# Routed feed-forward stages as one block each, and a sparse attention output summed in four parts

## The chip, the cores and the metric
The kernel runs on one core of one Trainium2 chip. The metric is device time in microseconds (us) of one execution. The core has five engines with queues of their own: TensorE (PE; its weight loads are listed as PEld), VectorE (DVE), ScalarE (ACT), GpSimd (POOL) and SyncE (SP), which issues most DMAs. They are ordered by semaphores alone.

## The reference
A perceiver with four layers. The state `x` is 16 batches of 64 latents of width 128, so 1024 tokens; the context is 16 x 1601 x 128. Each layer adds a cross-attention, a self-attention and a feed-forward stage to `x`, each on a normalised copy. Four of the twelve stages matter here; everything is float32.

- **Feed-forward 1**: 8 experts, width 128 to 512 to 128 with ReLU and biases. Softmax of the router's logits, the best two experts of each token, their probabilities shared out to sum to one, and a capacity of 256 places an expert: a token whose place in an expert's queue is beyond it loses that expert.
- **Feed-forward 2**: 8 experts that are one 128 x 128 matrix and a bias each; the best two of each token are summed with weight one.
- **Feed-forward 3**: 8 experts 128 to 128 to 128 with SiLU, weighted by the router's probability (the best two), and a shared gated expert whose output is scaled by a sigmoid of each token.
- **Cross-attention 3** (sparse): 16 heads of 8; of each query's 1601 scores only the 32 largest take part in the softmax.

```
first two experts:  p = softmax(logits); keep = top-2(p)
out = x + sum_e coef[token, e] * (act(xn @ W1[e] + b1[e]) @ W2[e] + b2[e])
```

## The kernel before
The whole state lives in on-chip memory: `c.x` is 128 partitions x 8 tiles x 128, `c.xn` the normalised copy, `c.xnT` its transpose. `perceiver` runs the twelve stages one after another. A stage is a row of blocks (`nc.Block()`): in a block each engine has its own list of instructions, and at a block's end all engines meet at a barrier. There is no planner: the order on each engine is the order in which the code was written, and waits on semaphores tie the lists together. `layernorm` is the first block of each stage; SP loads the stage's small weights in it and waits for all of them before the barrier.

**Routed stages.** `stage_l1_ffn` is norm, `turn_all` (transposes of the router's weights and of the first bias), `route`, `add_expert_bias` and `experts`. `route` is one block: TensorE makes logits for all 1024 tokens (L2500), VectorE finds the coefficients in some 20 dependent small steps on 128 x 64 (L2521 to L2562, `Link` makes each wait for the one before), ACT takes one Exp between (L2515), and with a capacity TensorE counts the picks between (L2508, L2509) and VectorE sums the counts over the tiles. `add_expert_bias` is two blocks: the coefficients are transposed one tile at a time, and multiplied by the bias rows (L2578), and VectorE adds the product (L2584). `experts` is one block with a hardware loop on each engine, two experts in an iteration. A *half* is one expert on 512 tokens: `up(k)` (L2640) makes C banks of hidden values, ACT applies the function (L2670), `down(k)` (L2649) makes the output, VectorE adds it to `x` weighted by the coefficient (L2696), four instructions. Weights lie in two slots, loaded by L2611 and L2613; a slot is loaded again once its expert is done. In the first stage the first weights are also transposed (L2635, copy by VectorE at L2686), and each expert's bias and coefficients are copied out for the loop (L2681, L2682). `stage_l2_ffn` transposes 8 matrices in `turn_all`, routes, adds the bias and then runs a block: TensorE multiplies a tile by all 8 matrices (L2752), two tiles ahead, and VectorE adds the 8 results one after the other (L2761). `stage_l3_ffn` routes, runs `experts` with C = 1, and then the shared expert in a block of its own (L2791 to L2813).

**Sparse cross-attention** (`topk_cross_attention`). 128 steps, each two heads of one batch. In step s VectorE searches the 32 largest of 1601 scores (`fold` L1144 and L1146, `find` L1160, `drop` L1165), ACT and GpSimd turn the scores of step s-1 into weights, and TensorE transposes and sums those of s-2, after the scores of s+1. `turn_u` (L946) transposes a step's normalised sum into bank `psZ`, and ACT copies it to `UT` (L1059). Every 16 steps two batches are complete: `sums` (L951) multiplies all 16 heads' `UT` by the output weights into the same bank, 32 instructions, and VectorE adds the result (`add`, L1183) right after it has inverted that step's sum (L1179). Steps 1 to 4 and 9 to 12 of each 16 also make the next batch's keys (L902, L987). The order of the products and of the add:

```
                        for q in range(4):
                            values(t, q)
                        if t and t % (2 * TB) == 0:
                            sums(t // (2 * TB) - 1)
```

Of the kernel before, what the change touches and what calls it, by code (L numbers as in the profile page):

```python
# [783 lines left out]
def topk_cross_attention(c, N, QT, WkT, bk):  # L784
# [9 lines left out]
    LISTS = 7  # L794
    with ExitStack() as st:
# [21 lines left out]
        UT = c.sb(st, "UT", [128, H, 2, S])  # L817
# [12 lines left out]
        slot = {use: u for u, use in enumerate(uses)}  # L830

# [26 lines left out]
        with nc.Block() as block:  # L858
# [25 lines left out]
            def _(pe):  # L884
# [63 lines left out]
                def sums(p):  # L948
                    pe.wait_ge(ut_ready, 2 * TB * (p + 1) + ONE)
                    for h in range(H):  # L950
                        last = pe.matmul(psZ[:, 128:256], UT[:, h, :, :], N[:, h, :], start=(h == 0),  # L951
                                         stop=(h == H - 1))
                    last.then_inc(y_ready, 1)
# [4 lines left out]
                for s in range(T + 2):  # L958
                    if s + 1 < T:
                        scores(s + 1)  # L960
                    t = s - 2
                    if t in keyed:
                        project(*keyed[t])
# [5 lines left out]
                    if t >= 0:  # L969
                        turn(t, 2)  # L970
                        turn(t, 3)
                        for q in range(4):
                            values(t, q)
                        if t and t % (2 * TB) == 0:
                            sums(t // (2 * TB) - 1)
                turn_u(T - 1)
                sums(NT - 1)

            @block.scalar
            def _(act):  # L980
# [73 lines left out]
                def copy_ut(t):  # L1054
                    p, b, n = t // (2 * TB), t // TB, t % TB
                    act.wait_ge(u_turned, t + 1 + ONE)
                    if t % (2 * TB) == 0 and p:
                        act.wait_ge(y_ready, p + ONE)
                    act.activation(UT[:, 2 * n:2 * n + 2, b % 2, :],  # L1059
# [76 lines left out]
            def _(dve):  # L1136
# [44 lines left out]
                def add(p):  # L1181
                    dve.wait_ge(y_ready, p + 1 + ONE)
# [4 lines left out]
                for s in range(T + 2):  # L1187
# [12 lines left out]
                    if s < T:  # L1200
                        find(s, 2, KP)
                    if s + 1 < T:
# [8 lines left out]
                add(NT - 1)  # L1211
                dve.wait_ge(y_added, NT + ONE)
# [1253 lines left out]
def route(c, st, Wr, br, weights, cap=None):  # L2466

    nc = c.nc
    coef = c.sb(st, "coef", [128, NT, E])
    with ExitStack() as s:
        p = c.sb(s, "p", [128, NT, E])
        rest = c.sb(s, "rest", [128, NT, E])
        first = c.sb(s, "first", [128, 2, NT, E])
        rank = c.sb(s, "rank", [128, NT, E])
        m = c.sb(s, "m", [128, 2, NT, 1])
        r = c.sb(s, "r", [128, NT, 1])
        tri = c.sb(s, "tri", [128, 128])  # L2480
        off = c.sb(s, "off", [128, 2, NT + 1, E])
        ps = c.ps(s, "logits", [128, NT * E])
        pc = c.ps(s, "counts", [128, 4, NT * E])
        made, order, logits, sub, expd = (c.sem(n) for n in ("made", "order", "logits", "sub", "expd"))
        picked, counted, done = c.sem("picked"), c.sem("counted"), c.sem("done")
        with nc.Block() as block:
            @block.gpsimd
            def _(pool):
                link = Link(pool, made)

                link(pool.iota(rank[:], pattern=[[0, NT], [-1, E]], base=E, channel_multiplier=0,
                               allow_small_or_imprecise_dtypes=True))
                link(pool.memset(tri[:], 1.0))
                link(pool.affine_select(out=tri[:], in_=tri[:], compare_op=ALU.is_ge, fill=0.0, base=0,
                                        pattern=[[1, 128]], channel_multiplier=-1))

            @block.tensor
            def _(pe):
                for t in range(NT):
                    last = pe.matmul(ps[:, t * E:t * E + E], c.xnT[:, t * 128:t * 128 + 128], Wr,  # L2500
                                     start=True, stop=True)
                last.then_inc(logits, 1)
                if cap:
                    pe.wait_ge(picked, 1 + ONE)
                    pe.wait_ge(made, 3 + ONE)
                    for k in range(2):
                        f = first[:, k].rearrange("p t e -> p (t e)")
                        pe.matmul(pc[:, k, :], tri[:], f, start=True, stop=True)  # L2508
                        last = pe.matmul(pc[:, 2 + k, :], c.ones[:], f, start=True, stop=True)  # L2509
                    last.then_inc(counted, 1)  # L2510

            @block.scalar
            def _(act):
                act.wait_ge(sub, 1 + ONE)
                act.activation(p[:], p[:], ACT.Exp).then_inc(expd, 1)  # L2515

            @block.vector
            def _(dve):
                link = Link(dve, order)
                dve.wait_ge(logits, 1 + ONE)  # L2520
                link(dve.tensor_copy(p[:].rearrange("p t e -> p (t e)"), ps[:]))  # L2521
                if br is not None:
                    link(dve.tensor_tensor(p[:], p[:], bc(br, [128, NT, E]), ALU.add))
                link(dve.reduce_max(r[:, :, 0], p[:], axis=X))
                dve.tensor_tensor(p[:], p[:], bc(r[:], [128, NT, E]), ALU.subtract).then_inc(sub, 1)
                dve.wait_ge(expd, 1 + ONE)
                link(dve.reduce_sum(r[:, :, 0], p[:], axis=X))
                link(dve.reciprocal(r[:, :, 0], r[:, :, 0]))
                link(dve.tensor_tensor(p[:], p[:], bc(r[:], [128, NT, E]), ALU.mult))
                link(dve.tensor_copy(rest[:], p[:]))  # L2530
                dve.wait_ge(made, 3 + ONE)
                for k in range(2):
                    f = first[:, k]
                    link(dve.reduce_max(m[:, k, :, 0], rest[:], axis=X))
                    link(dve.tensor_tensor(f, rest[:], bc(m[:, k], [128, NT, E]), ALU.is_equal))
                    link(dve.tensor_tensor(f, f, rank[:], ALU.mult))
                    link(dve.reduce_max(r[:, :, 0], f, axis=X))
                    link(dve.tensor_tensor(f, f, bc(r[:], [128, NT, E]), ALU.is_equal))
                    if k == 0:
                        link(dve.scalar_tensor_tensor(out=rest[:], in0=f, scalar=-2.0, in1=rest[:],  # L2540
                                                      op0=ALU.mult, op1=ALU.add))
                if cap:

                    link(dve.tensor_tensor(r[:], m[:, 0], m[:, 1], ALU.add))
# [1030 lines left out]
```

## Time and profile before

| | |
|---|---|
| time, median of 3 runs | 4493.35 us (4491.63 to 4499.15) |
| the profiled execution's time | 4484.32 us |
| its span | 4482.6 us |
| busy share PE / DVE / ACT / POOL | 79% / 76% / 63% / 23% |
| mean granted TensorE clock | 0.912 of 2.4 GHz |
| feed-forward 1, from its norm to the next one | 1552.2 to 1729.6 us |
| feed-forward 2 | 2634.9 to 2693.3 us |
| sparse cross-attention, steps | about 2740 to 4240 us |
| feed-forward 3, to its last add | 4391.7 to 4477.0 us |

The profile is one execution, recorded by the hardware. Times of rows count from its span's start. The shares are averages over stages that are bound by different engines, so each stage has to be read by itself. A TensorE row is one hardware instruction: a float32 product is two of them. "Idle before" is how long the engine stood before a row's work, and what released it.

### The profile page before, as it was taken

How to read it: one execution, taken by the hardware profiler on the slowest of the kernel's cores; microseconds unless marked ns; L12 is line 12 of the kernel's file. 1: busy time of each engine (PE TensorE's matmuls, PEld its weight loads, DVE VectorE, ACT ScalarE, POOL GpSimd, SP SyncE). 2: the span in 40 equal slices, each digit the busy share in tenths (PEclk: the TensorE clock that was granted, in tenths of full speed). 3: DMA queues.
4: the chain of work that ended last, by engine and by line, in shares of the span. 5: the costliest groups of instructions: out<-in, count | busy, mean ns of one | idle time of the engine just before them, and what ended most of it. 6: DMA issues, size and time to landing. Idle time of an engine off the chain costs nothing. (4 is left out here: it accounts for less than half of the span.)

```text
span 4482.6 us, 71801 instructions
## 1 busy us (share of the span) xinstructions
PE 3525.9 (79%) x25855; PEld 2832.6 (63%) x25855; DVE 3418.4 (76%) x5489; ACT 2808.6 (63%) x4637; POOL 1033.6 (23%) x1056
## 2 busy tenths in 40 slices
PE   6345649999999677999999875777777777777796
PEld 3334338999998355999999753555555555555574
DVE  5675767777777624877777557999999999999643
ACT  3113517666666423666666425999999899999732
POOL 0000502121110201211211002444434443444310
PEclk9556769999999788999999887999999999999897
DMA  8752011011110102101110001000000000000000
GB/s 277 95 84 78 5 48 36 30 42 33 30 38 8 26 28 65 38 30 30 40 35 23 22 6 40 16 16 30 16 16 16 16 30 16 16 16 8 20 4 17
DMA packets 186564, 161.25 MB, mean 36 GB/s; under 512 B 8220, under 2 KB 174316, under 8 KB 186220
## 3 DMA queue, kind: packets, MB, share of 16 engines
q1 hardware_dynamic: 182828, 142.83, 12.1%
q10 hardware_dynamic: 3392, 13.93, 0.9%
q8 instruction: 203, 3.33, 0.3%
q14 instruction: 141, 1.16, 0.1%
HBM read 127.36 MB, written 20.20 MB: 33 GB/s over the span
## 5 line engine op out<-in xcount | busy, mean ns | idle before, releaser
L538 PEld LDWEIGHTS psU<-ctxN,ST 128*128 128x128 f32 x6656 | 853.7, 191 | 98.2 <-issue 39.4
L538 PE MATMUL psU<-ctxN,ST 128*128 128x129 f32 x6656 | 868.1, 275 | 20.4 <-issue 20.4
L1160 DVE MAX8 top<-pairs 128x8 f32<-128x801 f32 (+1 forms) x512 | 709.2, 1406 | 4.5
L624 ACT ACTIVATE ST<-ST 128x512 f32<-128x512 f32 (+1 forms) x832 | 513.1, 625 | 167.1 <-DVE ST L726 163.2
L1125 POOL TENSOR_TENSOR P<-P,EX 128x1601 f32<-128x1601 f32 x128 | 459.5, 3590 | 582.5 <-ACT P L1035 582.5
L935 PE MATMUL psU<-ctxN,PT 128*128 128x129 f32 (+1 forms) x3328 | 432.0, 281 | 202.0 <-ACT PT L1043 202.0
L726 DVE TENSOR_TENSOR ST<-ST,psB 128x512 f32<-128x512 f32 (+1 forms) x832 | 556.4, 677 | 3.2 <-PE psB L557 3.2
L712 DVE TENSOR_TENSOR psA<-psA,ST 128x512 f32<-128x512 f32 x640 | 446.8, 698 | 137.5 <-ACT ST L616 70.4
L935 PEld LDWEIGHTS psU<-ctxN,PT 128*128 128x128 f32 (+1 forms) x3328 | 394.3, 193 | 226.3 <-ACT PT L1043 226.3
L1165 DVE MATCH_REPLACE8 pairs<-top,pairs 128x801 f32<-128x801 f32 (+1 forms) x384 | 482.4, 1256 | 0.0
L913 PE MATMUL psS<-KT,stat 128*128 128x512 f32 (+1 forms) x1024 | 390.4, 525 | 15.9 <-DVE pairs L1144 15.1
L526 PE MATMUL psS<-statL,ctxH 128*128 128x512 f32 x832 | 393.2, 473 | 5.0 <-ACT ST L619 2.5
L616 ACT ACTIVATE ST<-psS,key_bias 128x512 f32<-128x512 f32 (+1 forms) x416 | 284.2, 683 | 145.2 <-PE psS L526 140.2
L619 ACT ACTIVATE ST<-psS 128x512 f32<-128x512 f32 (+1 forms) x416 | 246.9, 593 | 165.9 <-PE psS L526 160.5
L923 PE MATMUL psT<-ident,P 128*128 128x128 f32 (+1 forms) x1664 | 256.6, 283 | 95.5 <-ACT KT L987 71.2
L526 PE MATMUL psS<-statH,ctxH 128*128 128x512 f32 x832 | 331.2, 398 | 0.0
L526 PE MATMUL psS<-statH,ctxL 128*128 128x512 f32 x832 | 328.0, 394 | 0.0
L913 PEld LDWEIGHTS psS<-KT,stat 128*128 128x128 f32 x1024 | 190.5, 196 | 212.1 <-issue 211.1
L923 PEld LDWEIGHTS psT<-ident,P 128*128 128x128 f32 (+1 forms) x1664 | 192.4, 144 | 166.0 <-ACT KT L987 85.4
L656 POOL CAST ctxH<-ctxM 128x1601 fp32r<-128x1601 f32 x30 | 45.6, 1521 | 1011.5 <-DVE ctxM L685 1011.5
L1043 ACT ACTIVATE PT<-psT 128x512 f32<-128x512 f32 (+1 forms) x512 | 240.7, 511 | 17.5 <-PE psT L923 17.5
L994 ACT ACTIVATE SS<-psS 128x1601 f32<-128x1601 f32 x128 | 192.4, 1503 | 74.2 <-PE psS L913 73.7
(502 smaller groups left out, 6261.4 us busy)
## 6 DMA issues: line engine op xcount, KB each, us to landing
ctxT<-ctxT_scratch SPq DMA_DIRECT2D x48, 800.5 KB, 4.7
ctxN<-in_ctx SPq DMA_DIRECT2D x48, 768.0 KB
ctxT_scratch<-trn ACTq DMA_DIRECT2D x16, 800.5 KB
nat<-in_ctx SPq DMA_DIRECT2D x16, 768.0 KB
dist_scratch<-dd SPq DMA_DIRECT2D x8, 800.5 KB
skewed<-in_ctx SPq DMA_DIRECT2D x8, 768.0 KB
ctx_late<-in_ctx SPq DMA_DIRECT2D x8, 768.0 KB
room<-skewed SPq DMA_DIRECT2D x28, 201.0 KB, 4.2
```

Of the source, the lines that this page charges most:

```text
L526: last = pe.matmul(psS[:, i % RING, :], x[:, u // 2 % 2, o:o + 128], q[:, p % 2, heads, queries], start=(n_pass == 0), stop=(n_pass == 2))
L538: last = pe.matmul(psU[:, q, 0:D + 1], ST[0:n, i % SLOTS, q * 128:q * 128 + 128], ctxN[0:n, j, k, 0:D + 1], start=(k == 0 and q % 2 == 0), ...
L616: act.activation(ST[0:n, i % SLOTS, :], psS[0:n, i % RING, :], ACT.Identity, bias=key_bias[0:n, col:col + 1]).then_inc(copied, 1)
L624: act.activation(ST[0:n, i % SLOTS, :], ST[0:n, i % SLOTS, :], ACT.Exp).then_inc(exp_done, 1)
L712: dve.tensor_tensor(psA[:], psA[:], cell, ALU.max).then_inc(folded, 1)
L726: dve.tensor_tensor(cell, cell, psB[0:n, :], ALU.subtract).then_inc(shifted, 1)
L913: last = pe.matmul(psS[:, o:o + w], stat[:, b % 2, 2 * n:2 * n + 2, :], KT[:, b % 2, o:o + w], start=True, stop=True)
L923: last = pe.transpose(psT[0:w, j, (k % 4) * 128:(k % 4) * 128 + 128], P[:, t % 2, o:o + w], c.ident[:])
L935: last = pe.matmul(psU[:, 0:D + 1], PT[0:w, t % 2, k, :], ctxN[0:w, t // TB % 2, k, 0:D + 1], start=(k == 0), stop=(k == NC - 1))
L1125: pool.tensor_tensor(P[:, j, :], P[:, j, :], EX[:, j, :], ALU.mult).then_inc(p_ready, 1)
L1160: dve.max(top[:, j, 8 * n:8 * n + 8], pairs[:, j, 0:width]).then_inc(listed, 1)
L1165: dve.match_replace(pairs[:, j, 0:width], top[:, j, 8 * n:8 * n + 8], pairs[:, j, 0:width], LOW).then_inc(listed, 1)
```

## The change
Each routed stage becomes the norm and one block, without a loop. `route` turns into a class, `Router`, whose parts are called from each engine's list. TensorE goes on with products of the first experts while VectorE finds the coefficients; the bias is an output like another one, in the middle of the list. ACT takes over the copies of transposed weights. Expert 0 and 1 of the first stage, and all of the last stage's, are loaded in the norm; the other six of the first stage at the start of the block, each with its own place and semaphore. `hT` has three slots for two. In the last stage the shared expert comes first, in two halves, and GpSimd multiplies its gate. In the second stage the adds start with the coefficients, and the bias is added after two tiles.

In the sparse attention the output of 16 heads is made in four parts of four heads. For the first seven batch pairs they are made in steps 5, 6, 7 and 13 of the next 16, ahead of that step's transposes; each is added by VectorE after the third search. `UT` is doubled, since it is still read while the next one is filled. The transpose of U in the same step waits for the add, which reads its bank. For the last pair the four parts follow each other at the end.

```
-    with ExitStack() as s:
-        p = c.sb(s, "p", [128, NT, E])
...
+class Router:
...
+    def choose(self, dve):
+        p, rest, first, m, r, off, wide = self.p, self.rest, self.first, self.m, self.r, self.off, [128, NT, E]
+        link = Link(dve, self.order)
+        dve.wait_ge(self.logits, 1 + ONE)
+        if self.br is None:
+            link(dve.tensor_copy(p[:].rearrange("p t e -> p (t e)"), self.ps))
+        else:
+            link(dve.tensor_tensor(p[:], self.ps.rearrange("p (t e) -> p t e", e=E), bc(self.br, wide), ALU.add))
...
+def add_weighed(dve, c, bank, half, weight, y_added):
+
+    for t in range(4):
+        tt = half * 4 + t
+        last = dve.scalar_tensor_tensor(out=c.x[:, tt, :], in0=bank[:, t * 128:t * 128 + 128], scalar=weight(tt),
+                                        in1=c.x[:, tt, :], op0=ALU.mult, op1=ALU.add)
+    last.then_inc(y_added, 1)
```

The first stage, norm and TensorE's and ACT's lists:

```
+        layernorm(c, [(g[:], d["L1_ffn_gate_w"]), (b1n[:], d["L1_ffn_fc1_b"].rearrange("e a (q p) -> (e a q) p", p=128)),
+                      (b2[:], d["L1_ffn_fc2_b"].rearrange("e a d -> (e a) d"))] + weights(0) + weights(1))
...
+                for e in range(2, E):
+                    for out, src in weights(e):
+                        sp.dma_start(out, src).then_inc(loaded[e], 16)
...
+                def up(i):
+                    e, half = i // 2, i % 2
+                    pe.wait_ge(copied, turn_use["w", e] + 1 + ONE)
+                    for q in range(C):
+                        if i:
+                            pe.wait_ge(h_ready, C * (i - 1) + q + 1 + ONE)
+                        pe.matmul(psH[:, q, :], w1T[:, e, q, :], c.xnT[:, half * 512:half * 512 + 512],
+                                  start=True, stop=True).then_inc(h_made, 1)
...
+                turn(("w", 0))
+                pe.wait_ge(small_copied, 2 + ONE)
+                route.make_logits(pe, Wr[:])
+                turn(("w", 1))
+                up(0)
+                up(1)
+                route.count(pe)
+                for i in range(UNITS):
+                    down(i)
+                    if i + 2 < UNITS:
+                        up(i + 2)
+                    if i % 2 == 0 and i // 2 + 2 < E:
+                        turn(("w", i // 2 + 2))
+                    if i == BIAS_FROM - 1:
+                        for half in range(2):
+                            turn(("coef", half))
+                        for half in range(2):
+                            bias(half)
...
+                copy(("w", 0))
+                act.wait_ge(small_copied, 2 + ONE)
+                copy(("w", 1))
+                route.exponentiate(act)
+                rectify(0)
+                rectify(1)
```

The second stage's and the last stage's TensorE lists:

```
+                route.make_logits(pe, Wr[:])
+                product(0)
+                product(1)
+                pe.wait_ge(route.coef_ready, 1 + ONE)
...
+                for t in range(2, NT):
+                    product(t)
...
+                last.then_inc(gates_made, 1)
+                route.make_logits(pe, Wr[:])
+                shared_up(0)
+                up(0)
+                shared_up(1)
+                up(1)
+                output(0)
+                output(1)
+                for i in range(UNITS):
+                    if i + 2 < UNITS:
+                        up(i + 2)
+                    output(2 + i)
```

The sparse attention:

```
+        summed = {PAIR * (p + 1) + n: (p, g) for p in range(NT - 1) for g, n in enumerate((5, 6, 7, 13))}
...
-                    if t % (2 * TB) == 0 and t:
-                        pe.wait_ge(y_added, t // (2 * TB) + ONE)
+                    if t + 1 in summed:
+                        p, g = summed[t + 1]
+                        pe.wait_ge(y_added, PARTS * p + g + 1 + ONE)
...
+                    if t in summed:
+                        sums(*summed[t], t - 1)
...
-                        if t and t % (2 * TB) == 0:
-                            sums(t // (2 * TB) - 1)
                 turn_u(T - 1)
-                sums(NT - 1)
+                for g in range(PARTS):
+                    sums(NT - 1, g, T)
...
-                        if s > 3 and (s - 3) % (2 * TB) == 0:
-                            add((s - 3) // (2 * TB) - 1)
...
                         find(s, 2, KP)
+                    if s - 2 in summed:
+                        add(*summed[s - 2])
```

## Rows read from the trace of the kernel before

**Rows 1.** Windows: us, busy (instructions) by engine, PEclk, DMA share, GB/s.
```profile
1552.00:1590.00 38.00, 14.84 (x60) 11.38 (x61) 17.52 (x86) 4.70 (x8) 0.74 (x3) 0.55 0.07 21
1590.00:1729.60 139.60, 121.42 (x672) 85.80 (x670) 24.42 (x86) 43.98 (x64) 0.00 (x0) 0.98 0.08 25
4408.00:4460.00 52.00, 37.41 (x160) 24.67 (x160) 19.02 (x72) 14.69 (x20) 0.00 (x0) 0.83 0.07 20
3300.00:3512.00 212.00, 157.10 (x938) 115.36 (x939) 207.78 (x259) 195.75 (x286) 91.23 (x96) 0.99 0.08 24
1100.00:1300.00 200.00, 197.73 (x1416) 181.80 (x1416) 158.17 (x256) 136.74 (x233) 41.23 (x29) 1.00 0.12 38
```

**Rows 2.** Timeline, feed-forward 1, routing: start, us, engine, line, operation, count [idle before].
```profile
1559.69 3.55 PE L2500 MATMUL logits<-Wr,xnT 128*128 128x8 f32 x16 [0.74 <-PEq L229]
1563.28 0.23 DVE L2521 COPY p<-logits 128x64 f32<-128x64 f32 x1 [4.11 <-PE logits L2500]
...
1568.88 0.07 DVE L2547 MEMSET off<- 128x8 f32 x1
...
1576.10 0.23 DVE L2562 TENSOR_TENSOR coef<-coef,p 128x64 f32<-128x64 f32 x1
...
1589.65 1.11 PE L2635 MATMUL psX<-ident,w1n 128*128 128x128 f32 x4 [5.38 <-DMA w2n<-in_L_ffn_fc_w]
```

**Rows 3.** Timeline, feed-forward 1, the experts' loop.
```profile
1591.64 6.04 PE L2640 MATMUL psH<-xnT,w1T 128*128 128x512 f32 x8 [0.88 <-DVE w1T L2686]
...
1628.10 3.69 PE L2640 MATMUL psH<-xnT,w1T 128*128 128x512 f32 x8 [2.04 <-DVE w1T L2686]
...
1652.43 7.31 PE L2649 MATMUL psY<-w2n,hT 128*128 128x128 f32 x64
...
1662.21 3.69 PE L2640 MATMUL psH<-xnT,w1T 128*128 128x512 f32 x8 [2.03 <-DVE w1T L2686]
...
1728.00 1.13 DVE L2696 SCALAR_TENSOR_TENSOR x<-psY,ce,x 128x128 f32<-128x128 f32 x4 [2.44 <-PE psY L2649]
```

**Rows 4.** Timeline, feed-forward 2: transposes, router, adds.
```profile
2641.40 3.38 PE L236 MATMUL turn<-ident,We 128*128 128x128 f32 x8
...
2649.21 0.23 DVE L2521 COPY p<-logits 128x64 f32<-128x64 f32 x1 [4.11 <-PE logits L2500]
...
2654.37 0.23 DVE L2560 TENSOR_TENSOR coef<-first 128x64 f32<-128x64 f32 x1
...
2668.10 24.68 DVE L2761 SCALAR_TENSOR_TENSOR x<-psE,coef,x 128x128 f32<-128x128 f32 x64 [4.31 <-PE psE L2752]
```

**Rows 5.** Timeline, feed-forward 3: a table load in the loop, the last adds.
```profile
4424.67 1.28 ACT L2670 ACT_TABLE_LOAD   x1 [3.23 <-DVE ce L2682]
4425.97 0.60 ACT L2670 ACTIVATE hT<-psH 128x512 f32<-128x512 f32 x1
...
4474.86 2.16 DVE L2813 SCALAR_TENSOR_TENSOR x<-psY,sg,x 128x128 f32<-128x128 f32 x8 [3.88 <-PE psY L2798]
```

**Rows 6.** Timeline, sparse attention: first and 125th reciprocal, an add, a turn of U.
```profile
2776.03 0.15 DVE L1179 RECIPROCAL li<-psU 128x1 f32<-128x1 f32 x1
...
2958.15 0.29 DVE L1183 TENSOR_TENSOR x<-x,psZ 128x128 f32<-128x128 f32 x1 [1.28 <-PE psZ L951]
2958.36 0.08 DVE L1165 MATCH_VALUE_LOAD pairs<-top,pairs 128x8 f32 x1
...
3109.67 1.83 DVE L1160 MAX8 top<-pairs 128x8 f32<-128x1602 f32 x1
3110.13 0.33 PE L946 MATMUL psZ<-ident,U 128*128 128x128 f32 x1 [0.97 <-ACT U L1051]
...
4209.48 0.15 DVE L1179 RECIPROCAL li<-psU 128x1 f32<-128x1 f32 x1
...
4235.55 3.84 PE L951 MATMUL psZ<-N,UT 128*128 128x128 f32 x32 [0.37 <-ACT UT L1059]
```

**Rows 7.** Source view of L2613: its eight 256 KB and eight 64 KB transfers.
```profile
DMA to landing us min/median/max: 1.8/2.6/4.9
```

**Rows 8.** The page's costliest groups: GpSimd's product in the sparse attention.
```profile
L1125 POOL TENSOR_TENSOR P<-P,EX 128x1601 f32<-128x1601 f32 x128 | 459.5, 3590 | 582.5 <-ACT P L1035 582.5
```

More of the change, by code:

```diff
@@ new lines, in rectify @@
+                def rectify(i):
+                    if i >= SLOTS:
+                        act.wait_ge(y_ready, place["unit", i - SLOTS] + 1 + ONE)
+                    for q in range(C):
+                        act.wait_ge(h_made, C * i + q + 1 + ONE)
+                        act.activation(hT[:, i % SLOTS, q, :], psH[:, q, :], ACT.Relu, bias=b1[:, i // 2, q:q + 1]
+                                       ).then_inc(h_ready, 1)
+                act.wait_ge(small_turned, 1 + ONE)
+                act.activation(Wr[:], small[:, 0:E], ACT.Copy).then_inc(small_copied, 1)
@@ new lines, in _ @@
+                act.activation(b1[:].rearrange("p e q -> p (e q)"), small[:, E:E + 32], ACT.Copy).then_inc(small_copied, 1)
+                copy(("w", 0))
[6 more added lines that the diff above has]
+                    if i + 2 < UNITS:
+                        rectify(i + 2)
+                    if i % 2 == 0 and i // 2 + 2 < E:
+                        copy(("w", i // 2 + 2))
+                    if i == BIAS_FROM - 1:
+                        for half in range(2):
+                            copy(("coef", half))
@@ L2744, in stage_l2_ffn, with _, product @@
         flat = WeT[:].rearrange("p e d -> p (e d)")
         with nc.Block() as block:
+            @block.gpsimd
+            def _(pool):
+                route.make_tables(pool)
             @block.tensor
             def _(pe):
[L2748 removed]
+                def product(t):
+                    pe.wait_ge(copied, 2 + ONE)
                     if t >= 2:
[L2750 removed]
+                        pe.wait_ge(added, E * (t - 1) + ONE)
@@ new lines, in _ @@
+                for t in range(2, NT):
+                    product(t)
+            @block.scalar
+            def _(act):
+                act.wait_ge(small_turned, 1 + ONE)
+                act.activation(Wr[:], small, ACT.Copy).then_inc(small_copied, 1)
+                for n in range(2):
+                    act.wait_ge(turned, n + 1 + ONE)
+                    act.activation(flat[:, 512 * n:512 * n + 512], psX[:, n, :], ACT.Copy).then_inc(copied, 1)
+                route.exponentiate(act)
+                for n in range(2):
+                    act.wait_ge(turned, use_at["coef", n] + 1 + ONE)
+                    act.activation(cT[:, 4 * n:4 * n + 4, :].rearrange("p t d -> p (t d)"), psX[0:E, n, :], ACT.Copy
+                                   ).then_inc(copied, 1)
@@ L2767, in stage_l3_ffn @@
 def stage_l3_ffn(c):
     nc, d = c.nc, c.dram
+    UNITS = 2 * E
+    SLOTS = 3
+    outputs = [("shared", 0), ("shared", 1)] + [("unit", i) for i in range(UNITS)]
     with ExitStack() as st:
@@ new lines, in shared @@
+                def shared(half):
+                    act.wait_ge(shared_made, half + 1 + ONE)
+                    act.activation(upper[:, half, :], psG[:, 1, :], ACT.Copy).then_inc(up_ready, 1)
+                    act.activation(gate[:, half, :], psG[:, 0, :], ACT.Silu).then_inc(silu_ready, 1)
+                route.exponentiate(act)
+                act.wait_ge(gates_made, 1 + ONE)
+                act.activation(sg[:], psg, ACT.Sigmoid).then_inc(gated, 1)
+                shared(0)
+                silu(0)
```

567 lines of the change are left out of this document (301 added, 266 removed).

## The prediction
> **What bounds the kernel now.** I read the windows view first, by stage. The first routed stage has two halves: up to 1590 us TensorE is busy 14.8 of 38 us at a granted clock of 0.55, and no engine is half busy; from 1590 to 1729.6 it is busy 121 of 139.6 us at 0.98, so there it is the bound, with holes [rows 1]. The last stage's experts are worse: 37 of 52 us at 0.83. The sparse cross-attention is bound by VectorE (208 of 212 us) [rows 1]. Then the timeline. In the routing part [rows 2] the reader sees a relay: logits, some 20 small VectorE steps, counts, coefficients, bias, and only then weights that are issued when the bias is added; the products that need none of this begin at 1591.64 [rows 3]. In the loop, two experts (four halves of 512 tokens) take 1662.21-1628.10 = 34.11 us [rows 3].
>
> **First routed stage (8 experts, 16 halves).** The new block starts later than the old routing, for the norm's block now waits for 1 MB of weights. A 256 KB transfer among four landed after 1.8 to 4.9 us [rows 7]. Now the first of four is issued at about 1553.3 (1552.2 and three small issues), the last 1.6 us later; with 4.5 us for the last I get 1559.3, and 0.4 us of barrier: 1559.7, where the small transposes stood at 1558.5. Cost 1.1 (bounds 0 and 3.5). The Trainium skill (DMA: Bandwidth & Descriptors, "Anatomy of one DMA — SWDGE (gpsimd) path") gives 2.0 us plus bytes over 436 GB/s, for 1 MB 4.4 us from the first issue; that would make this cost nothing, and what it says is for another way of issuing.
>
> From there TensorE: small transposes and the first expert's (1.5), logits 3.55 [rows 2], to 1564.7. A turn of four is 1.1 at the low clock [rows 2]. VectorE needs 1568.88-1563.28+0.1 = 5.7 us to its picks, but ACT now copies expert 1's weights and loads the Exp table (1.28 [rows 5]) after them, so Exp ends at 1568.0 instead of 1565.8: picks at 1572.7. Meanwhile TensorE turns expert 1 (1.1), does half 0 (8 instructions, 6.04 us while the clock rises [rows 3]; I take 4.7, it has worked since 1559.7) to 1570.5 and half 1 (3.43: eight instructions in 3.69, less about 0.26 in which the next work already runs [rows 3]), then counts (1.1): 1575.1. After that it has 16 downs of 3.57 (64 instructions in 7.31, so 32 in 3.57 with the last one's tail off [rows 3]) = 57.1, 14 ups of 3.43 = 48.0, 6 turns of 0.47 = 2.8, and the bias: coefficients turned in two pieces through one bank, two ACT copies between, 16 small matmuls, 4.5 us in all. Sum 112.4, end 1687.5, last add 1.3: 1688.8. Before, the last add ended at 1729.1 [rows 3]. **Gain 40.** Coefficients take 5.3 us from the counts (1571.0 to 1576.10+0.23 [rows 2]), so they arrive at 1580.5; the first two outputs have a bank each, the third is wanted only at about 1586, so they hide. The activation pass is 4 x 0.86 = 3.4 of a half's 7.0 us and the adds 1.1: neither is late. The remaining 3 MB are wanted from 1582 on. Bounds: 34 (the loop's 4.5 us of hole per 34 stays in part) and 43.
>
> **Second routed stage.** No new weights in the norm. The eight transposes no longer alternate with copies (3.38 us with them [rows 4], 2.2 without), and one block edge of 0.9 us goes, so logits end 2.1 us earlier; the bias joins the copy (one step of 0.26). Coefficients: 2652.3 instead of 2654.6 [rows 4]. Two products are ready by then. The old kernel began its 64 adds at 2668.10, after the bias relay; they take 24.68 us, back to back [rows 4]. New: adds from 2652.35, two tiles 6.2, bias 1.45 (two of 0.69, ready since 2655.5 or at the low clock 2658), six tiles 18.5: 2678.5 against 2692.8. **Gain 14** (11 to 16).
>
> **Last stage.** Its norm also loads 1 MB more: start 1.1 later. Gates (3.5 at the low clock) and logits 3.55 come first, 4399.8 to 4406.9. ACT: Exp 4408.0, Sigmoid's table and op 4409.5, Copy, Silu's table, Silu 4412.2, first half 4412.85. The second shared half waits for it: 4412.3 to 4415.2, up 4416; GpSimd's two products are 1.15 us each (3590 ns for 1601 columns [rows 8]), the last ends at 4417.2, its output at 4418.2. Then 14 ups of 0.86 and 16 downs of 0.89 (a quarter of the first stage's) = 26.3, end 4444.5, add 1.3: 4445.8. Old end: 4474.86+2.16 = 4477.0 [rows 5]. That is 31; the clock was 0.83 in the old loop [rows 1] and may be late here too, which I charge at 3 us. **Gain 28** (20 to 32). What goes: four table loads before the loop's first half, on the path each time [rows 5], the separate shared expert, the loop's restart. Of tables the Trainium skill (ScalarE: Activation LUTs, "What ACT_TABLE_LOAD costs") says that each switch pays a drain of about 1.38 us beside the load. Here the load is 1.28 us and the next operation starts 0.02 us after its end [rows 5]; with the drain the new exposed switches (one in the first stage, two in the last) would cost some 4 us more.
>
> **Sparse cross-attention.** Per step VectorE needs 11.29 us. From the first to the 125th reciprocal there are 4209.48-2776.03 = 1433.45 us in 124 steps [rows 6]: 33.5 above 124 x 11.29. I listed all 124: seven batch ends hold 31.7 of it, 3.4 to 6.3 each (the add waits for 32 matmuls, 1.28 us in [rows 6], later scores and their copy come late), three of the eight other key batches 0.55 each, which will be so at some of the seven too (1.4). Removed: 31.7-1.4 = 30.3. Added: 28 adds on VectorE, each worth 0.21 (the add at 2958.15 is followed by the next at 2958.36) = 5.9. The eight matmuls of a part are 0.96 us of a TensorE that isn't the bound. But the turn of U in that step now waits for the add, which stands behind the third search: TensorE does it at 3110.13, the search runs from 3109.67 for 1.83 [rows 6]; so it waits 1.3 us, with the part's matmuls before it 1 to 2.4 late in all. Queued behind it are two transposes, the value products and the next scores. The value products wait for ACT anyhow, at 1.5 us; so at most 0.9 gets through to ACT, which has 0.65 us to spare a step, and I charge 1.8 us over all. The tail grows: the last 32 matmuls (3.84, one add [rows 6]) become four rounds, 3 x 0.6 = 1.8. **Gain 21**; bounds 5 (if 0.6 per part reaches VectorE) and 27.
>
> **Sum.** 40+14+28+21 = 103 us. The profiled execution took 4484.3 (span 4482.6); it would become 4381. The three timed runs have their median 9.0 higher, so I say 4390. About 9 us (0.2%) is what timing this kernel can tell from no change.
>
> **Rivals.**
> A. *The holes stay.* The halves chain through TensorE, ACT and VectorE so that the old per-half pace remains: 34.11/4 = 8.5 instead of 7.0, and 52/16 = 3.2 in the last stage [rows 1] instead of 1.75. Then 16 x 1.5 and some 14 x 1 are not won: gain 65, time 4428. For it: the old trace shows the waits. Against: each of those waits is for the copy of turned weights, for a table or for the loop's edge, and all three leave.
> B. *The split sums hurt.* The wait for the add goes through whole: 28 x (2.4+0.96-0.65) = 76 us against 24 won: the attention loses 50, time 4461. For it: ACT is 92% busy, so it can't catch up much [rows 1]. Against: the 1.5 us for which the value products stand idle anyhow.
> C. *The clock* (the other side). The block's products run at 1.2 GHz (granted 0.5, as in the routing parts) instead of 2.4: each us of the 113 and 26 costs one more. All of it: 139 us, time 4493-103+139 = 4529. It decides from 103 us of product work at the low level. Against: at 1100 to 1300 TensorE is busy 197.7 of 200 us at 1.00, and the clock fell only after idle stretches; the new block has fewer of those [rows 1, 2].
> D. *Only the stages' overlap counts*: weights late or the picks waited for in TensorE's queue at 1574; each some 3 us, inside the range.
>
> **Chances.** The forecast with its bounds 0.78 (by itself 4372 to 4415), A 0.10, B 0.06, C 0.02, the rest, something better than my bounds, 0.04. The range, which takes in A, is 4368 to 4430. Faster 0.96, same 0.015, slower 0.025.
>
> **What would show it.** First transposes of the first stage near 1559.7 and its span, norm to norm, 177 down to 137; the count matmuls after half 1; one hole of about 3 us at the bias and none between halves. Second stage: adds from 2.3 us earlier than the old coefficients, 58.4 down to 44. Last: last add 28 us earlier relative to its norm, halves 1.75 us apart. Attention: reciprocals 11.29 to 11.5 apart at batch ends, with no add waiting; U's turn late in 28 steps. Wrong if halves stay 8.5 apart, if the granted clock is at 0.5 inside a block, or if steps with a part run over 11.8.

## The result, and the profile after

| | before | after |
|---|---|---|
| median on one chip (4 runs each) | 4492.49 us (4487.59 to 4499.15) | 4376.1 us (4370.77 to 4377.72) |
| profiled execution | 4484.32 us | 4374.6 us |
| first routed stage, norm to next norm | 177.4 | 136.1 |
| second routed stage | 58.4 | 43.3 |
| sparse attention, first reciprocal to last add | 1463.7 | 1439.8 |
| last stage, norm to last add | 85.3 | 54.65 |
| everything else, to the last add | 2692.3 | 2694.2 |

The ratio is 0.9741, with a 95% interval of 0.9729 to 0.9754: 116 us faster by the medians, 109.7 by the two profiled executions. 4390 was forecast, in 4368 to 4430.

The timeline of TensorE in the first stage of the kernel after, against [rows 2, 3]:

```profile
1559.99 0.24 PE L2681 MATMUL bank<-ident,g 8*128 8x8 f32 x1 [1.88 <-PEq L153]
...
1561.22 3.42 PE L2509 MATMUL bank<-Wr,xnT 128*128 128x8 f32 x16
...
1565.38 9.22 PE L2657 MATMUL psH<-xnT,w1T 128*128 128x512 f32 x16
1574.44 0.33 PE L2517 MATMUL bank<-first,tri 128*128 128x64 f32 x2
...
1575.28 3.79 PE L2670 MATMUL psY<-w2n,hT 128*128 128x128 f32 x32
...
1604.24 0.60 PE L2648 MATMUL psX<-ident,coef 128*8 128x128 f32 x4
1605.65 0.60 PE L2648 MATMUL psX<-ident,coef 128*8 128x128 f32 x4 [0.81 <-ACT coefT L2711]
1606.18 2.05 PE L2678 MATMUL psY<-b,coefT 8*128 8x128 f32 x16
1608.15 3.84 PE L2670 MATMUL psY<-w2n,hT 128*128 128x128 f32 x32
```

A bracket is time in which the engine stood. From 1560 to the end of the stage TensorE has one, 0.81 us, at the coefficients' second turn. The first expert's products (9.22 us for two halves) run while VectorE makes the picks; before, they came at 1591.64 [rows 3]. VectorE's coefficients and its last adds in the same stage:

```profile
1572.66 0.07 DVE L2554 MEMSET off<- 128x8 f32 x1
1580.58 0.23 DVE L2568 TENSOR_TENSOR coef<-coef,p 128x64 f32<-128x64 f32 x1
...
1687.43 1.13 DVE L2577 SCALAR_TENSOR_TENSOR x<-psY,coef,x 128x128 f32<-128x128 f32 x4 [2.45 <-PE psY L2670]
```

The second stage, where VectorE goes from the coefficients to the last add without a wait, against [rows 4]:

```profile
2610.93 0.23 DVE L2565 TENSOR_TENSOR coef<-first 128x64 f32<-128x64 f32 x1
2611.19 6.14 DVE L2839 SCALAR_TENSOR_TENSOR x<-psE,coef,x 128x128 f32<-128x128 f32 x16
...
2617.37 1.29 DVE L2850 TENSOR_TENSOR x<-x,psX 128x512 f32<-128x512 f32 x2
...
2618.69 18.50 DVE L2839 SCALAR_TENSOR_TENSOR x<-psE,coef,x 128x128 f32<-128x128 f32 x48
```

The last stage (its norm begins at 4313.41): the second shared half waits for the gate's Silu, the second output for GpSimd; then TensorE makes an output each 1.75 us. Against [rows 5]:

```profile
4334.25 1.98 PE L2900 MATMUL psG<-xnT,gu 128*128 128x512 f32 x4 [1.74 <-ACT gate L2951]
...
4338.75 1.16 PE L2921 MATMUL psY<-down,gate 128*128 128x128 f32 x8 [0.77 <-POOL gate L2890]
...
4340.61 1.05 PE L2921 MATMUL psY<-w,hT 128*128 128x128 f32 x8
...
4342.36 1.05 PE L2921 MATMUL psY<-w,hT 128*128 128x128 f32 x8
...
4364.47 3.59 DVE L2577 SCALAR_TENSOR_TENSOR x<-psY,coef,x 128x128 f32<-128x128 f32 x12 [0.63 <-PE psY L2921]
```

The windows, first stage's first 36 us and its remaining 100, then the last stage's two parts; against [rows 1] the clock in the experts' part is 1.00, and TensorE is busy 97.6 of 100 us:

```profile
1552.91:1589.00 36.09, 31.48 (x141) 21.73 (x142) 15.95 (x81) 16.15 (x27) 0.74 (x3) 0.81 0.40 118
1589.00:1689.00 100.00, 97.58 (x591) 72.88 (x589) 17.14 (x58) 37.83 (x57) 0.00 (x0) 1.00 0.00 1
...
4313.41:4342.00 28.59, 20.54 (x80) 14.59 (x81) 11.53 (x56) 11.30 (x18) 3.25 (x5) 0.69 0.16 44
4342.00:4368.00 26.00, 24.49 (x146) 18.13 (x144) 17.66 (x64) 7.76 (x13) 0.00 (x0) 1.00 0.00 1
```

The sparse attention, a step with a part: part, search, add, and the turn of U behind it, against [rows 6].

```profile
2958.62 1.11 PE L960 MATMUL psZ<-N,UT 128*128 128x128 f32 x8
...
2960.38 1.83 DVE L1170 MAX8 top<-pairs 128x8 f32<-128x1602 f32 x1
2962.13 0.27 DVE L1196 TENSOR_TENSOR x<-x,psZ 128x128 f32<-128x128 f32 x1
...
2962.54 0.30 PE L951 MATMUL psZ<-ident,U 128*128 128x128 f32 x1 [1.94 <-DVE x L1196]
...
2963.22 3.44 PE L939 MATMUL psU<-ctxN,PT 128*128 128x129 f32 x26
```

The waits view for VectorE over the steps, of the kernel before and then after (what it waited for: us in total, times, longest):

```profile
DVE inv_span L1173 <- POOL span L1110: 14.8, 28, 3.1
DVE x L1183 <- PE psZ L951: 9.7, 7, 3.1
DVE pairs L1146 <- ACT SS L994: 8.2, 7, 1.2
```

```profile
DVE inv_span L1183 <- POOL span L1120: 3.2, 9, 1.5
```

These three waits, most of them at the batch ends, came to 32.7 us and are gone but for 3.2. In the 124 steps alone, without the last ones (a wait of 3.1 before, of 1.5 after), they went from 29.6 to 1.7. The 125th reciprocal comes 1407.8 us after the first (1433.45 before). 27 of the 28 steps with a part lie in that stretch and take 11.49 instead of 11.29; eight others take 11.55 and one 11.41.

### The profile page after: what moved, and what is told of

Its sections match the earlier page's. It is cut to its first block and busy times, and to the rows that moved or that the text cites. A ratio compares the mean times of both kernels' runs of the same rounds, so it can differ in the third digit from the quotient of the medians.

```text
span 4372.8 us, 71369 instructions
## 1 busy us (share of the span) xinstructions
PE 3492.3 (80%) x25855; PEld 2823.6 (65%) x25855; DVE 3406.9 (78%) x5454; ACT 2810.9 (64%) x4654; POOL 1036.8 (24%) x1058
## 5 line engine op out<-in xcount | busy, mean ns | idle before, releaser
L1029 ACT ACTIVATE sides<-SS,top 128x1601 f32<-128x1601 f32 x128 | 208.1, 1626 | 33.9 <-DVE top L1170 33.8
```

## The experiments
They were run on several chips, each beside the kernel before; ratios are to that. "Stages" are read in each one's trace as in the table above: first / second / sparse / last. Seven executions have the four parts and the add in its place (the changed kernel three times, and the four experiments in which this part is the same); "the seven" below are these.

**The sparse change alone.** The kernel before, with only the four-part sum:

```
+        summed = {PAIR * (p + 1) + n: (p, g) for p in range(NT - 1) for g, n in enumerate((5, 6, 7, 13))}
...
+                    if s - 2 in summed:
+                        add(*summed[s - 2])
```

> The kernel before with the sparse attention's change alone. My sum gives this part 21 us, and the trace of after 22.7 us between the norms; the routed stages stay at 177.4, 58.4 and 85.3 us. I expect 4470 us against 4492 (ratio 0.9950), with the 28 waits of U's turn (2 us each) not seen in VectorE's steps of 11.49 us. Rival (the split sums hurt, and the gain that the trace of after shows between those norms came from somewhere else): ratio 1.000 or above.

Measured: 4458.28 us, ratio 0.9925 (0.9908 to 0.9941), span 4459.8 against 4482.6: 22.8 less. Stages 177.6 / 58.3 / 1438.2 / 86.1: the routed ones are the old ones, and the sparse one has its whole gain, 25.5 us for 23.9 in the full change. So the sparse part doesn't lean on the routed ones. By the medians it is 30.6 us faster, more than the 22 expected: the ratio 0.9950 lies outside the interval. The profiled execution of before is the fastest of its kernel, so differences of spans to it come out small.

**No overlap of routing and products.** One wait in each of the three lists of TensorE:

```
                 turn(("w", 1))
+                route.count(pe)
+                pe.wait_ge(route.coef_ready, 1 + ONE)
                 up(0)
                 up(1)
-                route.count(pe)
```

> The changed kernel, but in all three routed stages TensorE waits for the coefficients before the first expert's products (in the first stage the counts come before them); one block, no loop, the early loads and the bias inside stay. My theory: the overlap alone is worth, in the first stage, up(0) at the coefficients instead of before them, 14.5 us; in the second 3.6 us for the first product at the low clock and 2 for the bias that is then late; in the last 5.6 us and some 3 of low clock. Sum 29 us, time 4405, and 58 us of the routed stages' 87 remain: they come from the loop, the block edges and the bias relay. Rival (the overlap is the whole of it, as the change's words have it): 87 us lost, time 4463.

Measured: 4402.28 us, ratio 0.9805 (0.9788 to 0.9821). Stages 153.2 / 47.8 / 1438.7 / 60.7: 17.1, 4.5 and 6.0 more than after, 27.6 together, for 29 expected. Its trace, TensorE in the first stage:

```profile
1575.10 0.69 PE L2517 MATMUL bank<-first,tri 128*128 128x64 f32 x2 [7.18 <-DVE off L2554]
...
1582.47 10.13 PE L2657 MATMUL psH<-xnT,w1T 128*128 128x512 f32 x16 [5.40 <-DVE coef L2568]
```

So running the products beside the routing is worth at most 27.6 of the 86.9 us that the three stages gained. It may be some 3 us less: 1.6 are 32 products behind the bias that ran at a low clock in this execution (5.47 us for 3.84, see the last section), and the changed kernel's last stage itself took 54.65 to 56.0. The other 59 stay gone with the wait in place. They belong to the rest of the rewrite: the loop's holes, the bias relay, the table loads and the block edges. No run separates these four.

**One sum instead of four parts**, at step 5:

```
-    PARTS = 4
+    PARTS = 1
...
-        summed = {PAIR * (p + 1) + n: (p, g) for p in range(NT - 1) for g, n in enumerate((5, 6, 7, 13))}
+        summed = {PAIR * (p + 1) + n: (p, g) for p in range(NT - 1) for g, n in enumerate((5,))}
```

> The changed kernel with the sparse output summed whole (32 matmuls, one add) but still moved to step 5 of the next 16. It tells the place of the sums from their splitting. My theory: the parts matter since 3.84 us of sums ahead of the transposes make ACT's copies late by more than its slack (about 1.2 us plus 0.9 regained in the step): VectorE loses about 2 us at each of seven places (14), saves 21 adds of 0.2 (4.2) and two or three tail rounds (2): about 8 us slower than the changed kernel, 4384 (4377 to 4390). Rival (place alone did it, splitting only adds work): 6 us faster, 4370.

Measured: 4379.85 us, ratio 0.9752 (0.9735 to 0.9768). From first to 125th reciprocal it takes 1410.1 us; the seven with four parts take 1406.0 to 1407.8. So one sum is 2 to 4 us slower there, though these steps have 20 adds of 0.2 fewer; over the whole stage it is 1.4 slower (1440.1 for a mean of 1438.7), for 8 expected. The seven steps with a sum take 11.92 to 12.93. But the reason isn't the one I had written, a delay that goes on through TensorE's queue. The timeline shows VectorE itself waiting for the 32 products, and U's turn done soon after:

```profile
2949.65 3.79 PE L960 MATMUL psZ<-N,UT 128*128 128x128 f32 x32
...
2953.47 0.29 DVE L1196 TENSOR_TENSOR x<-x,psZ 128x128 f32<-128x128 f32 x1 [0.96 <-PE psZ L960]
...
2954.15 0.27 PE L951 MATMUL psZ<-ident,U 128*128 128x128 f32 x1
```

In the kernel after, a part of 8 is done 1.5 to 3.5 us before its add begins. A sum of 32 isn't: VectorE waits 0.3 to 1.1 us for it at each of the seven places, 5.1 together.

**The add later in the step**, behind the next fold and drop of VectorE (2.8 us), so that U's turn waits longer:

```
-                    if s - 2 in summed:
-                        add(*summed[s - 2])
                     if s + 1 < T:
                         fold(s + 1, False)
                     if s < T:
                         drop(s, 2, KP)
+                    if s - 2 in summed:
+                        add(*summed[s - 2])
```

> The changed kernel with VectorE's add of a part put 2.8 us later in its step, behind the next fold and the third drop. U's turn then waits about 4.9 us instead of 2.0. My theory: 2.0 is hidden because the value products stand idle for ACT anyway, 4.9 is not; each of 28 steps passes 2 to 3 us to VectorE: sparse attention 60 us longer (40 to 90), span 4433. Rival (TensorE has a quarter of its time free, so a wait of 5 us in 28 steps is absorbed too): no change, span 4373.

Measured, from one run: 4411.62 us. The 124 steps take 1440.2 us, 33.6 more than the mean 1406.6 of the seven, 1.2 for each part. The stage is 36.4 longer, less than the 40 to 90 expected. The chain that rival B described is there to be read:

```profile
2955.11 0.27 DVE L1196 TENSOR_TENSOR x<-x,psZ 128x128 f32<-128x128 f32 x1
...
2955.52 0.45 PE L951 MATMUL psZ<-ident,U 128*128 128x128 f32 x1 [3.91 <-DVE x L1196]
...
2956.83 4.89 PE L939 MATMUL psU<-ctxN,PT 128*128 128x129 f32 x26
...
2964.51 1.51 ACT L1004 ACTIVATE SS<-psS 128x1601 f32<-128x1601 f32 x1 [3.06 <-PE psS L917]
...
2966.05 0.99 DVE L1156 TENSOR_TENSOR pairs<-psS,SS 128x801 f32<-128x801 f32 x1 [1.30 <-ACT SS L1004]
```

The add, U's turn after a stand of 3.9 us, the value products, the scores, ACT's copy, and then VectorE waits. But the delay alone doesn't do it. The granted clock is 1.00 before this stand and 0.68 and 0.64 in the 5 us stretches from 2952 and 2957 on, and the 26 value products take 4.89 us. Another late turn, in the same trace, where the clock stayed at 1.00:

```profile
3426.76 0.30 PE L951 MATMUL psZ<-ident,U 128*128 128x128 f32 x1 [3.87 <-DVE x L1196]
...
3427.44 3.07 PE L939 MATMUL psU<-ctxN,PT 128*128 128x129 f32 x26
...
3435.14 0.97 DVE L1156 TENSOR_TENSOR pairs<-psS,SS 128x801 f32<-128x801 f32 x1
```

Nothing waits there, and the step takes 11.49 us and the next one 11.29. All 27 late turns within the 124 steps sort this way. After 18 of them the value products ran wholly or partly at the lower clock (3.9 to 5.0 us), and each time VectorE waited 1.0 to 1.3 us in the next step, which took 12.6 to 12.9. After nine they took 3.07, and the next step took 11.3 to 11.5 (seven of the nine lie in a step that had already become longer). The like cases are six stands of 3.9 us (3.86 to 3.88): after four the clock came down and the next step took 12.6, after two it didn't and the next step took 11.3. The other way round, the seven have 29 turns with the add in its place and the value products partly at the lower clock (4.2 to 4.7 us), and no step became longer. So VectorE pays where the late add and the low clock come together. In the changed kernel the place of the add keeps the first of them away.

**Two parts of eight heads**, at steps 5 and 13.

> The changed kernel with the sparse output in two parts of eight heads (added in steps 5 and 13) for four of four. My theory now is one of a threshold: the delay that a part puts on the turn of U costs nothing as long as it stays under what the value products' own wait covers. From the runs so far: no leak at 8 matmuls and the add after the third search; 1.1 us a step at 32 matmuls (24 x 0.12 = 2.9 more); 1.25 us a step with the add 2.8 us later; so some 1.5 to 1.8 us are still free, and 8 more matmuls (0.96 us) fit. Then it is faster: 14 fewer adds of 0.20 = 2.8, and two fewer rounds at the end of 0.7 = 1.4, together 4.2 us; median near 4372, sparse part from the last norm before it 1719.1 down to 1714.9, no step over 11.8. Rival, a smooth leak (a share of each us of delay reaches VectorE): 14 steps of 0.35 more = 5 us, which eats the gain; same time as the changed kernel.

Measured: 4374.93 us, ratio 0.9739 (0.9723 to 0.9755). The 124 steps take 1403.9 us (and 1403.9 and 1404.9 in two later kernels with two parts) against 1406.6: 2.7 less, for 2.8 expected (2.3 in the mean of the three), and none over 11.8. But it didn't put the question that it was built for. U's turn comes 3.37 us after its step's reciprocal, in every step with a part, with four parts and with two (once 3.63), since VectorE's add releases it in both. The eight further products fill time in which TensorE stood: it waits 0.7 us in each of 14 steps for 2.0 in each of 28. So no delay was added, and the smooth leak isn't tested here; the two clean cases of the run before, late and without a loss, speak against it.

The end gained nothing: first reciprocal to last add is 1436.1 for a mean of 1438.7 in the seven, which is the steps' gain. From the last reciprocal to the last add it is 6.2 us for 7.6, the 1.4 expected; but in all three executions with two parts the last 26 value products took 4.0 to 4.5 us, for 3.1 to 3.8 in the seven, at a mean granted clock of 0.63 to 0.67 in the 6 us before the last reciprocal (0.72 to 0.76). Why the clock is lower there stays open. The median moved by 1 us, within what timing can tell.

**The big weights loaded in the block**, not in the norm, in the first stage (shown) and in the last:

```
-                      (b2[:], d["L1_ffn_fc2_b"].rearrange("e a d -> (e a) d"))] + weights(0) + weights(1))
+                      (b2[:], d["L1_ffn_fc2_b"].rearrange("e a d -> (e a) d"))])
...
-                for e in range(2, E):
+                for e in range(E):
...
-                turn(("w", 0))
                 pe.wait_ge(small_copied, 2 + ONE)
                 route.make_logits(pe, Wr[:])
+                turn(("w", 0))
```

> The changed kernel with the big weights of the first and last routed stage loaded at the start of their block, not in the norm (which every engine waits for); the first stage's logits come ahead of the first expert's transposes, and expert 1's come after half 1. Theory (the norm waits for the last of its transfers): the block starts 0.8 us earlier in the first and 1.05 us earlier in the last stage, and the weights land 2 to 5 us later, behind the logits' 3.5 us, so the first stage, norm to norm, takes 135.2 us for 136.1, and the last one, norm to last add, 53.6 for 54.65. Rival: the transfers were never what ended the norm, or they come late for the first transposes; then both stages take what they took, or 1 to 2 us more.

Measured, from one run: 4373.48 us. Last stage 53.66, as expected to 0.1. First stage 136.57, no gain: its block begins 6.3 us after the norm for 7.1, but the 0.8 is given back, since the transposes no longer cover the copies. TensorE stands 0.35 before the logits and 0.69 before the first product:

```profile
1557.98 3.58 PE L2509 MATMUL bank<-Wr,xnT 128*128 128x8 f32 x16 [0.35 <-ACT b L2723]
...
1563.19 9.44 PE L2656 MATMUL psH<-xnT,w1T 128*128 128x512 f32 x16 [0.69 <-ACT w1T L2708]
```

**Silu before the copy, up(1) before shared_up(1)** in the last stage.

```
+                up(1)
                 shared_up(1)
-                up(1)
```

> The changed kernel with two pairs exchanged in the last stage: ScalarE applies Silu to the gate before it copies the other half, and TensorE makes the first expert's half 1 before the second shared half. Theory: TensorE's path at the start goes through the gate's Silu, as it waits for the shared half's bank to be free; the copy (0.6 us) and the 0.85 us of up(1) leave that path, so norm to last add becomes 52.7 to 53.4 for 54.65. Rival: the outputs' start is set by GpSimd's two gate products, which then come no earlier: 54.65 as it was.

Measured, from one run: 4373.43 us; last stage 54.8, where six executions with that stage unchanged have 54.65 to 56.0. The rival was right: the wait moved from ACT's Silu (1.74) to GpSimd's second product, which came no earlier.

```profile
4336.83 1.16 PE L2921 MATMUL psY<-down,gate 128*128 128x128 f32 x8 [1.70 <-POOL gate L2890]
```

**All three edits**, and **the changed kernel again** on the same chip.

> The changed kernel with all three edits together: two parts for four, the big weights loaded in the blocks, Silu first in the last stage. If the gains add up (4.2 + 0.9 + 1.05 + 1.5), it is 7.6 us under the changed kernel: 4368 us, ratio to the kernel before 0.9724. If only the parts help, 4372; if nothing helps, 4376 and the ratio 0.9741.

> The changed kernel itself once more, on the same chip as the kernel with all three edits: 4376 us, ratio 0.974. It tells how far two runs of one kernel lie apart, stage by stage, against which differences of some us have to be held.

Measured: 4369.42 us (4368.59 to 4374.55), ratio 0.9733 (0.9720 to 0.9747), against 4377.88 (4375.52 to 4380.66), ratio 0.9748 (0.9735 to 0.9761). No run of the one lies among those of the other, and the medians are 8.5 us apart, though the two ratios' intervals overlap. Their stages, 137.3 / 43.95 / 1436.0 / 53.4 and 139.2 / 43.3 / 1438.7 / 54.8, differ by 5.3 in sum, and the stages that are the same in both by as much again. The first stage of the changed kernel took 139.2 this time for 136.1: 2.8 of it is a fall of the clock (last section), so the edits themselves explain some 2.5 us, for 7.6 expected: 2.7 in the sparse stage and 1.4 in the last, less 0.9 in the first and 0.6 in the second, which no edit touches (it takes 43.3 us in six executions of the new form and 43.9 in four).

**The version the runs spoke for**: two parts; the last stage's weights in its block, Silu first, but shared_up(1) again before up(1); the first stage as in the changed kernel, with the coefficients turned in two places:

```
                     down(i)
+                    if i in (3, 4):
+                        turn(("coef", i - 3))
                     if i + 2 < UNITS:
                         up(i + 2)
```

> What the runs so far speak for: two parts in the sparse attention; the last stage's big weights loaded in its block, Silu ahead of the copy there, but the second shared half again before the first expert's half 1; the first stage loads in its norm as in the changed kernel, and its coefficients are turned one piece after down(3), the other after down(4), with a product between, so that TensorE never stands (before: 0.81 us), the bias one half later. Theory: first stage 135.3 (136.1 to 136.5 in the executions where the clock kept its level), last stage 52.8 (53.66 with the loads moved, and GpSimd's second gate product now some 0.9 earlier), sparse part 2.7 less as in the two runs with two parts: together 6 us under the changed kernel, its ratio to the kernel before 0.9733, like that with all three edits. Rival on the clock: what makes it fall behind the bias in some executions is the 0.81 us in which TensorE stands; then this one keeps its level (granted clock 1.0 in the 10 us behind the bias) and is up to 3 us better in some of its executions.

> The changed kernel a third time, on the same chip: 4376 us, ratio 0.9745. In the first routed stage either 136.1 to 136.5 us with the clock at its upper level behind the bias, or some 139.3 with it at 0.72 in the 10 us behind it, as in two of the executions so far.

Measured: 4373.71 us (4367.81 to 4377.31), ratio 0.9737 (0.9724 to 0.9750), against 4375.4 (4372.87 to 4381.71), ratio 0.9746 (0.9733 to 0.9760). The edited stages are what was expected, 135.3 / 43.9 / 1436.5 / 52.9 for 136.4 / 43.3 / 1439.3 / 56.0 of the changed kernel beside it; the time is 1.7 us under it, for 6 expected. The second turn stands without a wait in front:

```profile
1605.05 3.73 PE L2670 MATMUL psY<-w2n,hT 128*128 128x128 f32 x32
1608.62 0.60 PE L2648 MATMUL psX<-ident,coef 128*8 128x128 f32 x4
1609.06 3.60 PE L2657 MATMUL psH<-xnT,w1T 128*128 128x512 f32 x8
```

Yet the profiled execution is no shorter (span 4374.8 for 4371.2): the last self-attention, untouched, took 158.0 us in it and 150.8 in the other, with a granted clock, in windows of 20 us from its second on, of 0.83, 0.91, 0.91, 1.00, 0.83 and 0.83 for 0.83, 0.91, 1.00, 1.00, 1.00 and 0.74. Three to six us in the edited stages are at the edge of what the times of whole executions resolve here; the intervals of both improved versions overlap that of the changed kernel. By stages they are better, by ratio it isn't shown.

## Why the prediction was right
- **First stage, 40 forecast, 41.3 measured.** The block began 7.1 us after the norm (7.5 forecast; 6.3 before): the weights in the norm cost 0.8 (1.1 forecast; of the 1.8 to 4.9 us that I gave a 256 KB transfer, 1.8 is a 64 KB one of the last stage, and those of 256 KB took 2.8 to 4.9). Picks at 1572.66 less 0.7 for the later norm, 1572.0 (1572.7 forecast), coefficients ready at 1580.1 (1580.5), counts after half 1, no hole between halves. The stand at the bias was 0.81 us, not 3: what I called a hole of 3 is work of 3.9 us from the first turn to the next output, 4.5 in the sum. Two halves took 9.22 where I had 4.7 + 3.43; the granted clock was 0.51 from 1561 to 1570. The parts of the sum were off by up to 1.1 us each, both ways, and their cancelling to 1 us is partly luck.
- **Second stage, 14 and 15.0.** VectorE's adds begin with the coefficients, the bias is ready in time, and the 24.6 us of adds have no wait in them.
- **Last stage, 28 and 30.6.** My sum was 31, and the 3 us that I took off for a late clock were not needed: 1.00 in the experts' part. Block start 1.05 later (1.1), 1.75 a half.
- **Sparse attention, 21 and 23.9.** In the forecast's terms: before, the 124 steps were 33.5 us above 124 x 11.29; after, they are 7.9 above it, and 27 x 0.20 = 5.4 of that are the adds (5.9 forecast for 28). So 33.5 - 2.5 = 31.0 was removed, for 30.3, and 31.0 - 5.4 = 25.6 is what the steps gained. The end cost 1.8, as forecast. The term that was too large is the 1.8 us for U's late turn, of which nothing reached VectorE. The turn stands 3.37 us after the reciprocal in all 28 steps, 1.2 later than the median of the others; TensorE's wait before it is 56.9 us in all, 2.0 each, and with 1.1 to 3.1 it goes beyond the 1 to 2.4 forecast. ACT had a little more room than I took: by [rows 1] it is idle 16.2 of 212 us, which is 0.87 a step and not 0.65.
- **The total.** The terms gave 103, the stages 110.8, the profiled executions 109.7. The time was 14 us under 4390, and half of that is the step from the profiled execution to the median: I added 9.0, since the profiled one of before was below its median by as much, and the one of after was 1.5 below its own. An offset of one execution isn't a property of the kernel.
- **Rivals.** A is refuted by the 1.75 and 7.0 us a half. B's price was not paid. The kernel with the late add paid 34 us of it in the 124 steps, but by a path that B doesn't name: only where the value products behind the late turn ran at the low clock. With the clock up, a wait of 3.9 us was absorbed. C, the clock inside the block, happened in small: see the last section. D's waits didn't occur; its title, that overlap alone counts, is wrong by the run without it: overlap is at most 27.6 of 86.9.

ScalarE's table in the first stage: the load before the Exp stands at 1566.31 for 1.28 us, and the operation starts at 1567.60.

```profile
1566.31 1.28 ACT L2523 ACT_TABLE_LOAD   x1
1567.60 0.26 ACT L2523 ACTIVATE p<-p 128x64 f32<-128x64 f32 x1
```

The drain of some 1.38 us that the Trainium skill (ScalarE: Activation LUTs, "What ACT_TABLE_LOAD costs") adds to each switch is not seen here either: 0.01 us between the two.

## What to carry to other kernels
Write a routed stage as one list for each engine, with products that need no routing placed where the routing waits: of what was won here, a third at most was the overlap, and two thirds went with the old form (its loop, relays, table loads and block edges, which no run separates). When a sum is split so that its add never waits, ask two things of each piece: is it finished when the adding engine arrives, and is what it delays behind slack. Both held for 8 and 16 products, and the first failed for 32. The second held with the add 2.8 us later too, as long as the clock stayed up, and failed each time it didn't: slack that is enough at the upper clock can be too little at the lower one. And judge an edit of a few us by its own stage, not by the span: untouched stages differ by 11 us from run to run.

## What the runs showed of the hardware that was not expected
In ten executions with the coefficients' turns back to back, TensorE stands 0.81 us and then does 16 small products on 8 rows. In seven of them the next 32 products take 3.84 us; in three they take 5.47, 6.42 and 6.47. In the windows of one of these three (the changed kernel again) the granted clock is 0.72 in the 10 us there, between 1.00 and 0.93: part of them at the lower of the two levels (1.2 of 2.4 GHz), after 30 us of unbroken work and the 0.81 us. Below the windows its timeline, where the 16 small products themselves take 2.64 us for 2.05:

```profile
1593.00:1603.00 10.00, 10.00 (x55) 6.84 (x55) 2.25 (x8) 4.18 (x7) 0.00 (x0) 1.00 0.00 0
1603.00:1613.00 10.00, 9.19 (x48) 7.55 (x47) 1.37 (x2) 2.85 (x5) 0.00 (x0) 0.72 0.01 2
1613.00:1623.00 10.00, 10.00 (x60) 7.80 (x60) 1.41 (x6) 3.23 (x5) 0.00 (x0) 0.93 0.00 0
```

```profile
1606.19 2.64 PE L2678 MATMUL psY<-b,coefT 8*128 8x128 f32 x16
1608.76 6.47 PE L2670 MATMUL psY<-w2n,hT 128*128 128x128 f32 x32
```

It costs 2.8 us of the stage (139.2 for 136.4). The same program with the same waits does it or not. Without the 0.81 us it wasn't seen, but that is one execution, and whether the stand or the small products bring it on stays open.
